# Contexts and weights that arrive transposed: four latent layers of cross-attention on one core

## The reference, cut to what matters

```python
# L0_xattn: 8 heads of 64; masked
xn, ln = layernorm(ctx, ln_x_g, ln_x_b), layernorm(x, ln_l_g, ln_l_b)
q, kv = ln @ Wq, concatenate([xn, ln], 1) @ Wkv
out = layernorm(softmax(mask(q k^T * scale)) v @ Wo, ln_o_g, ln_o_b)
# L1_xattn: 16 heads of 64, on the raw context
q, k, v = x @ W_q, ctx @ W_k, ctx @ W_v
out = softmax(q k^T / 8) v @ W_o + b_o
# L1_ffn: 8 experts, silu(h1) * h2
scores = einsum('btd,ed->bte', x, gate_w); h12 = einsum('btd,ehd->bteh', x, w12)
# L2_xattn: 1 head of 128, on the raw context (keys and values)
out = softmax((x Wq + bq) (ctx Wk + bk)^T / sqrt(128)) (ctx Wv + bv)
# L3_xattn: 8 heads of 64, rotary keys
xn, ln = layer_norm(ctx, gamma_x, beta_x), layer_norm(x, gamma_l, beta_l)
k = concatenate([rope(xn @ Wk), ln @ Wk], 1); v = concatenate([xn, ln], 1) @ Wv
out = softmax(ln Wq k^T / 8) v @ Wo
```

## Time and profile before

| | us |
|---|---|
| median of 3 runs (2805.92 to 2808.92) | 2806.31 |
| the profiled execution | 2797.42 |
| its span | 2795.6 |
| L0_xattn, 0 to 509 | 509.0 |
| L1_xattn, 644.5 to 1461 | 816.5 |
| L1_ffn, 1493.5 to 1600 | 106.5 |
| L2_xattn, 1600 to 1716 | 116.0 |
| L3_xattn, 1899 to 2651 | 752.0 |
| the other seven stages together | 495.6 |

### The profile page before, as it was taken

How to read it: one execution, slowest core, us unless ns; L and a number is a source line. 1 busy time by engine, 2 the same in 40 slices (tenths; PEclk the granted TensorE clock), 3 DMA queues, 4 the chain that set the end, 5 groups by cost and what they waited for, 6 DMA issues and landing times. The chain is left out here.

```text
span 2795.6 us, 44841 instructions
## 1 busy us (share of the span) xinstructions
PE 2617.1 (94%) x16865; PEld 2195.2 (79%) x16865; DVE 1780.7 (64%) x3733; ACT 1627.8 (58%) x2865; POOL 1402.9 (50%) x1111
## 2 busy tenths in 40 slices
PE   5999999898999999999988888997999999999878
PEld 4899998686999999999987766785677777777647
DVE  7888885455555555555544545527888888888572
ACT  4888886335766666666643344434666666666433
POOL 1877875111766666666720062204666756566240
PEclk9999999999999999999999999999999999999999
DMA  3333231022011111101004041202000000000000
GB/s 113 95 86 108 73 97 37 15 58 63 25 38 35 36 36 36 36 24 37 24 7 135 1 118 32 61 1 80 25 13 25 14 25 25 14 25 2 3 1 8
DMA packets 222577, 117.88 MB, mean 42 GB/s; under 512 B 21368, under 2 KB 217633, under 8 KB 222369
## 3 DMA queue, kind: packets, MB, share of 16 engines
...
## 5 line engine op out<-in xcount | busy, mean ns | idle before, releaser
L873 POOL TENSOR_TENSOR L_xattn_held<-L_xattn_held,L_xattn_shift 128x512 f32<-128x512 f32 (+1 forms) x613 | 762.8, 1290 | 285.1 <-ACT L_xattn_shift L794 285.0
L590 PEld LDWEIGHTS L_xattn_acc<-L_xattn_rows,L_xattn_held 128*128 128x128 f32 (+2 forms) x5120 | 621.0, 192 | 34.4 <-DVE L_xattn_mixed L976 8.8
L590 PE MATMUL L_xattn_acc<-L_xattn_rows,L_xattn_held 128*128 128x129 f32 (+2 forms) x5120 | 630.4, 276 | 5.2 <-DVE L_xattn_mixed L976 5.2
L997 DVE TENSOR_TENSOR L_xattn_running<-L_xattn_ring,L_xattn_running 128x512 f32<-128x512 f32 (+1 forms) x384 | 264.2, 688 | 269.1 <-PE L_xattn_ring L572 257.3
L784 ACT ACTIVATE L_xattn_held<-L_xattn_held 128x512 f32<-128x512 f32 (+2 forms) x640 | 400.4, 631 | 0.2
L1642 POOL TENSOR_TENSOR L_xattn_projected<-L_xattn_along,L_xattn_crossed 128x512 f32<-128x512 f32 (+1 forms) x256 | 271.5, 1071 | 256.1 <-DVE L_xattn_crossed L1709 254.0
L777 ACT COPY L_xattn_held<-L_xattn_ring 128x512 f32<-128x512 f32 (+1 forms) x416 | 243.3, 585 | 227.7 <-DVE L_xattn_running L997 193.2
L570 PE MATMUL L_xattn_ring<-L_xattn_queries_hi,L_xattn_keys_hi 128*128 128x512 f32 (+2 forms) x640 | 281.3, 440 | 3.4 <-DVE L_xattn_keys_lo L901 2.0
L572 PE MATMUL L_xattn_ring<-L_xattn_queries_hi,L_xattn_keys_lo 128*128 128x512 f32 (+2 forms) x640 | 253.6, 396 | 0.0
L571 PE MATMUL L_xattn_ring<-L_xattn_queries_lo,L_xattn_keys_hi 128*128 128x512 f32 (+2 forms) x640 | 253.0, 395 | 0.0
L1346 PE MATMUL L_xattn_sums<-L_xattn_probT,L_xattn_rows 128*128 128x256 f32 (+2 forms) x896 | 242.8, 382 | 0.6 <-ACT L_xattn_mixed L1531 0.6
...
## 6 DMA issues: line engine op xcount, KB each, us to landing
...
```

The lines of the kernel that those rows point to most:

```text
L590: mm = nc.tensor.matmul(acc[:, c // 2, c % 2 * WIDE:(c % 2 + 1) * WIDE], held[0:n, u % 2, k, c * P:(c + 1) * P], rows[0:n, b % 2, k, :], s ...
L873: nc.gpsimd.tensor_tensor(tile, tile, shift[0:keys_of_tile[k]], ALU.subtract).then_inc(shifted, 1)
L997: seen = nc.vector.tensor_tensor(most, bank, most, ALU.max)
```

## The change

The host passes, beside the arrays of before, transposed copies (`..._turned`, last two axes swapped) of the context and of the weights of L0_xattn, L1_xattn, L1_ffn and L2_xattn that are used with their width on the partitions.

- L0_xattn: weights loaded turned; the means and inverse deviations of each batch's rows are stored to DRAM (`context_statistics`). `peak_wide` is gone here and in L1_xattn: PE reads `peak` as a broadcast.
- L1_xattn: the context is loaded turned (128x1601) into `first_loads_fresh`; ACT rounds and DVE splits from there, with no PSUM bank. Behind the split DVE normalises the chunk in place (subtract, multiply) with two rows of statistics that SP loads as a broadcast, and SP stores the result (`context_turned`), waits for that store, and loads the next context.
- L1_ffn: w12, w3 and the gate loaded turned; POOL rounds and splits w12.
- L2_xattn: keys loaded turned beside the rows; no transposes and copies of them, no copy on POOL.
- L3_xattn: `context_turned` is loaded into `staged`; ACT applies gain and shift in place and rounds. POOL scales `xhat` into `rows` of the next batch at t = 3 and shifts it at t = 0. No `gained`.

```diff
@@ L0_xattn: SP
             def next_xhat(b):
                 sp.wait_ge(xhat_ready, len(CTX_CHUNKS) * (b + 1))
+                with nc.allow_non_contiguous_dma("a row of statistics"):
+                    for n, source in enumerate((mean_var[:, b % 2, :, 0], crstd[:, b % 2, :])):
+                        sp.dma_start(core.ctx_stats[b, n].rearrange("(k p) -> p k", p=P), source).then_inc(stats_stored, 16)
                 if b + 2 < BATCHES:
                     move_context(raw[:, b % 2], w_ctx, b + 2, ctx_loaded[b % 2])
...
@@ L1_xattn: SP
-                move_context(fresh, w_ctx, 1, ctx_loaded[1])
+                sp.dma_start(fresh[:], core.w["ctx_1024_turned"][1]).then_inc(ctx_loaded[1], 16)
                 load_rows(1)
+                sp.wait_ge(w_kept, QK_JOBS)
                 for b in range(BATCHES - 1):
+                    for c, (c0, n) in enumerate(CTX_CHUNKS):
+                        if b or c >= 2:
+                            sp.wait_ge(turned_normal, len(CTX_CHUNKS) * b + max(c - 1, 0))
+                        sp.dma_start(stats_rows[c % 2][:, :, 0:n], core.ctx_stats[b + 1, :, c0:c0 + n].partition_broadcast(P))\
+                            .then_inc(stats_loaded[c % 2], 16)
+                    sp.wait_ge(turned_normal, len(CTX_CHUNKS) * (b + 1))
+                    sp.dma_start(core.ctx_turned[b + 1], fresh[:]).then_inc(turned_stored, 16)
+                    sp.wait_ge(turned_stored, 16 * (b + 1))
                     if b + 2 < BATCHES:
-                        sp.wait_ge(spare_free, CHUNK_DONE[b + 1, len(CTX_CHUNKS) - 1])
-                        move_context(fresh, w_ctx, b + 2, ctx_loaded[b % 2])
+                        sp.dma_start(fresh[:], core.w["ctx_1024_turned"][b + 2]).then_inc(ctx_loaded[b % 2], 16)
                     if b >= 1:
                         load_rows(b + 1)
...
@@ L1_xattn: PE, scores
-                    pe.wait_ge(spare_free, CHUNK_DONE[b, k // TURNS])
+                    if normed:
+                        pe.wait_ge(spare_free, CHUNK_DONE[b, k // TURNS])
+                    else:
+                        pe.wait_ge(ctx_split, len(CTX_CHUNKS) * (b - 1) + k // TURNS + 1)
...
@@ L1_xattn: DVE, split_context
+                dve.wait_ge(ctx_rounded, len(CTX_CHUNKS) * (b - 1) + c + 1)
+                split_chunk(b, c, None).then_inc(ctx_split, 1)
+                c0, n = CTX_CHUNKS[c]
+                part = fresh[:, c0:c0 + n]
+                dve.wait_ge(stats_loaded[c % 2], 16 * (2 * (b - 1) + c // 2 + 1))
+                nc.vector.tensor_tensor(part, part, stats_rows[c % 2][:, 0, 0:n], ALU.subtract)
+                dve.drain()
+                nc.vector.tensor_tensor(part, part, stats_rows[c % 2][:, 1, 0:n], ALU.mult).then_inc(turned_normal, 1)
...
@@ L3_xattn: SP, PE, ACT, POOL
-                if b + 3 < BATCHES:
-                    sp.wait_ge(gained_ready, b + 3)
-                    load_context(b + 3)
+                if b + 2 < BATCHES:
+                    sp.wait_ge(keys_split, NC * (b + 1))
+                    load_turned(b + 2)
+                    sp.wait_ge(rows_scaled, b + 1)
+                    load_context(b + 2)
...
-                        elif between is not None and not last:
-                            turn_context(*after, between)
...
-                bank = take()
-                emptied(nc.scalar.copy(turned[:, c % 2, 0:n], bank[:, 0:n]))
+                part = staged[:, c0:c0 + n]
+                if c == 0:
+                    act.wait_ge(staged_loaded, 16 * (pair * 2 + parity))
+                nc.scalar.activation(part, part, ACT.Identity, bias=shift_col[:], scale=gain_col[:])
...
-                    if t == R - 2 and not no_context:
-                        scale_context(b + 2, parity)
-                    if t == R - 1 and not no_context:
-                        shift_context(parity)
+                    if t == 0 and b:
+                        shift_rows(b)
+                    if t == R - 1 and not last:
+                        scale_rows(b + 1)
...
```

526 lines of the change are left out of this document (182 added, 344 removed).

## The result

| | before | after |
|---|---|---|
| median of 4 runs, us | 2806.11 (2803.92 to 2808.92) | 3134.57 (3130.98 to 3141.31) |
| ratio, 95% interval | | 1.117 (1.115 to 1.120) |
| span of the profiled execution | 2795.6 | 3134.7 |
| mean granted clock | 0.982 | 0.926 |

A forecast was written before the change was run, and what follows sets the result against it. TensorE was taken to bound the four xattn stages; -25 (L1_xattn), -26 (L3_xattn), -19 (L2_xattn), -7.5 (L1_ffn) and -3 (L0_xattn) sum to -81 us: 2716 profiled, 2725 us median. The range was 2705 to 2778.

The forecast's parts named there:

- the price of the small stores: L0_xattn: 3328 4-byte stored elements per batch cost 11.5 ns of one engine each, as column loads do; nothing lost.
- the slack of 3 us: L0_xattn: estimated delay per batch that the raw context's early load, DVE's idle pieces and POOL's wait can hide.
- Rival (d): L0_xattn: statistics stores at 56 ns per element delay 12.6 us, lose 134 us, total 2859, slower than before; chance 0.05.
- three groups of weight transposes: L0_xattn: three groups of four go, 1.3 us, plus up to 2 us of PSUM copies; -3 us.
- The term of the transposes: L1_xattn: 46 groups of context transposes, 19.8 us, plus weight transposes and waits go; together 24.4, say -25 us.
- so about 2 x (3 x 0.69 + 0.2) = 4.5 us ... I count nothing: L1_xattn: DVE's subtract and multiply add about 4.5 us per batch; the 1.4 us delay per pair counted as nothing.
- the ring of score banks: L1_xattn: score banks run some tiles ahead, so a normalising pair delaying the running maxima by 1.4 us costs nothing.
- 15 x 1.76: L3_xattn: a tile with two groups of context transposes shortens from 12.13 to 10.37 us in 15 batches; -26 us.
- rival (c): L3_xattn: DVE is already the bound, so only 10 of the 26 us come; total 2741; chance 0.08.
- 2.77 us, in 7 of the 8 steps: L2_xattn: a step shortens from 12.24 to 9.47 us without its 26 transposes; -19 us.
- Hidden behind an expert's ten us: L1_ffn: the split moved to POOL, 1.2 us twice, costs nothing; the stage gains 7.5 us.
- rival (a): L2_xattn: loads bound the stage, a step takes 11.3 us instead of 9.5, 11 us given back; total 2736; chance 0.12.

The follow-up runs named there:

- stores_one: Kernel before, plus one store of 1664 single 4-byte elements per L0_xattn batch ahead of the raw context on SP's queue: L0_xattn 645.6 us, +136.
- stores_two: Kernel before, plus two stores of 128x13 single 4-byte elements per L0_xattn batch ahead of the raw context: L0_xattn 770.5 us, total 3059.19.
- loads_two: Kernel before, plus two loads of 128x13 single 4-byte elements per L0_xattn batch in the same queue place: L0_xattn 527.7 us, +18.5.
- turned_from_first: Changed kernel without statistics or L1_xattn normalising; L0_xattn's ACT copies out the normalised turned context and SP stores it: 2757.85 us, ratio 0.986 to before.
- last experiment: L1_xattn's normalising replaced by L0_xattn storing the turned context, plus POOL's L1_ffn w12 splits held until products two experts earlier finish: 2755.49 us, ratio 0.984 to before.

## Why the prediction was wrong

**L0_xattn, forecast -3, came +254.** The step that failed is the price of the small stores, "I take the first price (same element size): nothing lost". The price was for loads, and as a packet's duration it was even too high: 8.4 ns was measured for the stores. The stretch it was taken from begins with 127 larger packets of another load; from 575.6 to 578.4, where the 4-byte loads of the kernel before are alone, they take 0.262 x 2.8 x 16 / 1467 = 8.0 ns:

```profile
q1 hardware_dynamic: 1467, 0.01, 26.2%
```

This would have led to the same "nothing lost". A packet's duration was the wrong quantity: the stores hold up what follows them, which their own mean duration does not show. The delay is some 17 us for each batch (raw loads mostly 42 to 45 us apart in place of 27), where the text had 3.4. The second step that failed is the slack of 3 us. `stores_one` and `stores_two` cost in proportion to their elements, so the slack is near nothing; one late transfer sets back DVE's queue, and PE's with it. Rival (d) had the place, the sign, and the deciding point of 8.8 us; its price of 12.6 us of delay gave 134 of the 254 us. It had a chance of 0.05, on the argument "against it: the loads of such elements at 11.5 ns", and `loads_two` shows what that argument was worth: +18.5 us for loads, +261 for stores. The rest of the term, three groups of weight transposes, is too small to be told: with them gone the stage took 509.0, 513.4 and 513.6 us in three kernels.

The rule quoted with the prediction (the Trainium skill, DMA: Bandwidth & Descriptors, Specifications: below 512 bytes the engine reads, modifies and writes) points the right way for elements of 4 bytes. No run here tests its threshold. Pieces of 52 bytes are below 512 too, but there are 256 of them in a batch and not 3328: at the 5 ns of the queue that an element costs they would come to 1.3 us a batch and 20 us in the stage, and 0 to 5 were seen. Of the separate elements 128 lie in each 512 bytes of DRAM. Whether the number of writes or their meeting in the same 512 bytes makes the stall, no run here parts.

**L1_xattn, forecast -25, came +107.** The term of the transposes was right: `turned_from_first` has 791.5 us, forecast 791. The step that failed is "so about 2 x (3 x 0.69 + 0.2) = 4.5 us ... I count nothing". Its two halves, measured: the operations take up to 1.8 us beside POOL, which makes 104 us (925.5 to 821.8); and even at 0.69 us they cost some 26 us in that place (821.8 to 795.9), where PE stood 1.6 us in each of 15 batches. The assumption that the ring of score banks covers a pair was argued from no row, and the wait that the text left out is another: the division of the finished sums (`mixed`) is queued on DVE behind the pairs as well, and PE stood 82.5 us for it, 2.4 before. In the pause of POOL both come to 2.8 us. The prediction's last sentence named this danger, "the normalising on DVE holds up the exponentials", but gave it neither a price nor a chance. A rival at 1.8 us for each of the 6 full operations of a batch, 1.1 more than 0.69, would have been 99 us in 15 batches, near the 104, but by luck: 56 of the 90 were stretched, by 56 us together, and the splits by 10. The rest of the 104 is not in DVE's durations; PE's matmuls at the lower clock took 38 of it.

What happens is told by the rows above: where an operation of DVE with both operands in SBUF meets one of POOL, one of the two waits for the other. The Trainium skill, SBUF — State Buffer, Who interferes with whom, says just this (a DVE instruction with two SBUF inputs contends with a GpSimd instruction that reads SBUF, and the one that comes second blocks); the trace agrees, 0.69 against 1.60 to 1.80 us for DVE, and 1.3 against 1.7 to 1.8 for POOL. The same page of the Trainium skill bears on what the change did to the split: before it read PSUM, and loading the context turned made it an operation with both operands in SBUF. The prediction passed over that. The split's group before, with one operand in a bank, and with POOL at work beside 42 of the 46:

```profile
L902 DVE TENSOR_TENSOR L_xattn_keys_lo<-L_xattn_spare,L_xattn_keys_hi 128x512 fp32r<-128x512 f32 x46 | 31.3, 681 | 0.2 <-issue 0.2
```

After, the 48 full splits took 903 ns on average.

**L3_xattn, forecast -26, came -17.** The step that was mis-sized is "15 x 1.76": it took the tiles around the long one to stay. The tile with two groups went from 12.13 to 10.41 us, as forecast. But the last tile of each batch grew, here from 9.74 to 10.50. The starts of scores on PE around such a last tile, before:

```profile
2089.64 2.97 PE L1320 MATMUL L_xattn_score<-L_xattn_projected,L_xattn_queries 128*128 128x512 f32 x8
2099.38 1.02 PE L1320 MATMUL L_xattn_score<-L_xattn_projected,L_xattn_queries 128*128 128x512 f32 x2
```

And after, of the tile that had the two groups (2463.56) and of a last one (2528.72):

```profile
2463.56 1.88 PE L1316 MATMUL L_xattn_score<-L_xattn_projected,L_xattn_queries 128*128 128x512 f32 x4
2473.97 1.88 PE L1316 MATMUL L_xattn_score<-L_xattn_projected,L_xattn_queries 128*128 128x512 f32 x4
...
2528.72 1.88 PE L1316 MATMUL L_xattn_score<-L_xattn_projected,L_xattn_queries 128*128 128x512 f32 x4
2539.22 1.02 PE L1316 MATMUL L_xattn_score<-L_xattn_projected,L_xattn_queries 128*128 128x512 f32 x2
```

Over the stage the mean of the tiles t = 1 fell from 12.2 to 10.6 us and of t = 2 from 10.7 to 10.5, and that of t = 3 rose from 10.6 to 11.3. That is near the lower bound of the text, "-15 if the tiles around it, which now catch up after a long one, lose that", and rival (c) in part. Between the first batch and the last no tile of the changed kernel is shorter than 10.39 us, about the floor that the text found for one tile; DVE is busy 85% of the stage. That DVE sets this floor is read from the rows, and no run tested it.

**L2_xattn, forecast -19, came -9.** An undisturbed step takes 9.5 us (2034.60 to 2044.10), as forecast. More than five us went in one wait, in the timelines of PE and SP:

```profile
2013.33 4.96 PE L1866 MATMUL L_xattn_score<-opening_keysT,L_xattn_queries 128*64 128x512 f32 x16 [5.48 <-DMA opening_keysT<-in_ctx_turned]
...
1998.81 0.48 SPq L3530 DMA_DIRECT2D ahead_rows_up<-in_L_attn_Wq_up_c  x1
...
2006.48 0.40 SPq L3551 DMA_DIRECT2D opening_keysT<-in_ctx_turned  x1
```

Ten loads of a later stage's weights, issued from 1998.81 on and the last at 2005.48, stand ahead of the keys in SP's queue. They stood there before too (from 1617.05), where the next context was not issued until 1627.92; a step of 12.2 us hid them, one of 9.5 does not. The failing step is "2.77 us, in 7 of the 8 steps": six of the seven distances took 9.9 to 14.9 us. This is not rival (a) in the main: the issue was late. Two more waits for keys, of 0.46 us at most, would fit (a). The scores behind the long wait took 4.96 us and those of the second step 4.11, against 2.92, at granted clocks of 0.58 and 0.70; the wait and this make 9 of the missing 10 us. No run moved the ten loads, so their part is read and not tested, and why the first step took 10.4 us was not tried.

**L1_ffn, forecast -7.5, came +2.** "Hidden behind an expert's ten us" failed for the splits that ran beside the router (last experiment): DVE and POOL meet there as in L1_xattn, PE waited 6.22 us, and its granted clock in the stage was 0.95, before 1.00. Pacing POOL gave back 4.9 us, L1_ffn and L2_xattn taken together; the rest of the 10 stays open.

**The sum.** The forecast's terms that rest on counted transposes and on distances in PE's timeline held within some us where nothing new stood in the way (`turned_from_first`: -43.5 of -81, with L3 and L2 as above and L1_ffn's loss). The two terms set to nothing, the small stores (257 us from forecast to result) and DVE's work (132), are 389 of the 420 us between the profiled execution as forecast, 2716, and as it came, 3136.6; L3_xattn, L2_xattn and L1_ffn are 9, 10 and 10. The range, built from prices of one engine or one packet alone, did not reach them.
